# A new order of work in the first attention stage: value columns as (e, r), z on ScalarE, the product in pieces, scores, shifted products and values in groups

## What is computed

```python
xn = _ln(x, g1, b1)
q = _lin(xn, Wq, bq).reshape(b, n, H, HD) / np.sqrt(HD)
k = _lin(xn, Wk, bk).reshape(b, n, H, HD)
score = softmax(einsum('bihd,bjhd->bhij', q, k), axis=-1)
v = _lin(xn, Wv, bv).reshape(b, n, R, HD)
out = einsum('bhij,bjrd->bihrd', score, v)
qv = _lin(xn, Wqv, bqv).reshape(b, n, H, 1, QK) / np.sqrt(QK)   # broadcast over R
comp = softmax(concatenate([qv, out], -1) @ Ws.T + bs, axis=3)   # over R
out = (comp * out).sum(axis=3).reshape(b, n, DIM)
```

## Time and profile before

| | us |
|---|---|
| median of three runs (1930.48 to 1957.68) | 1944.45 |
| the profiled execution | 1938.15 |
| its span | 1936.4 |
| TensorE busy (share of the span) | 1592.3 (82%) |
| VectorE busy | 1485.4 (77%) |
| GpSimd busy | 835.4 (43%) |
| ScalarE busy | 771.2 (40%) |
| mean granted clock of TensorE, of full speed | 0.917 |

### The profile page before, as it was taken

One profiled execution on the slowest core, in us unless ns is written; L12 is line 12 of the kernel. 1 busy time (PEld: TensorE's weight loads), 2 busy tenths in 40 slices (PEclk: granted clock), 3 DMA queues, 4 the chain that ended last, 5 costly groups with the idle time before them and its releaser, 6 DMA issues. The chain is left out here.

```text
span 1936.4 us, 45555 instructions
## 1 busy us (share of the span) xinstructions
PE 1592.3 (82%) x13604; PEld 1346.0 (70%) x13668; DVE 1485.4 (77%) x3618; ACT 771.2 (40%) x1665; POOL 835.4 (43%) x1052
## 2 busy tenths in 40 slices
PE   5899898898989898999476654888888888888887
PEld 3788888888888888889355543666666666666665
DVE  4668888888888888887488865777787787777774
ACT  1345555555555555556122212333333333333331
POOL 3445554544554554453366643334333344333330
PEclk9899999999999999999689987999898999888896
DMA  3322212222122212221333312232222222222220
GB/s 110 109 85 93 79 66 70 72 80 72 65 76 73 75 64 72 73 77 42 87 94 98 98 46 73 92 99 91 90 94 97 93 92 94 90 87 88 87 93 31
DMA packets 178621, 158.08 MB, mean 82 GB/s; under 512 B 9458, under 2 KB 160114, under 8 KB 178547
## 3 DMA queue, kind: packets, MB, share of 16 engines
q1 hardware_dynamic: 178546, 157.16, 24.6%
HBM read 113.09 MB, written 44.04 MB: 81 GB/s over the span
## 5 line engine op out<-in xcount | busy, mean ns | idle before, releaser
L600 PE MATMUL a_bank<-a_vp,a_prob 128*128 128x96 f32 x4096 | 544.7, 277 | 0.3 <-ACT a_prob L457 0.3
L600 PEld LDWEIGHTS a_bank<-a_vp,a_prob 128*128 128x128 f32 x4096 | 511.3, 196 | 16.7 <-ACT a_prob L457 8.6
L633 DVE TENSOR_REDUCE a_nmax<-a_bank 128x2 f32<-128x512 f32 x512 | 331.8, 686 | 123.6 <-PE a_bank L527 123.0
L457 ACT ACTIVATE a_prob<-a_bank 128x512 f32<-128x512 f32 x512 | 306.0, 598 | 180.0 <-PE a_bank L582 170.9
L527 PE MATMUL a_bank<-a_k_st,a_q_st 96*128 96x256 bf16 x1024 | 207.8, 286 | 7.5 <-DVE a_nmax L633 5.5
L1698 DVE TENSOR_REDUCE c_nmax<-c_bank 128x4 f32<-128x512 f32 x256 | 166.8, 684 | 51.8 <-PE c_bank L1510 50.1
L1540 PE MATMUL c_o_bank<-c_vb,c_prob 128*128 128x96 f32 x1024 | 181.4, 303 | 30.0 <-DVE c_ad L1823 29.2
L582 PE MATMUL a_bank<-a_q_st,a_k_st 120*128 120x256 bf16 x1024 | 202.2, 279 | 0.0
L335 POOL TENSOR_TENSOR a_prod<-a_ov,a_wgt 128x2048 f32<-128x2048 f32 x32 | 119.0, 3719 | 144.5 <-DVE a_wgt L706 131.8
L1414 ACT ACTIVATE c_prob<-c_bank 128x256 f32<-128x256 f32 x256 | 98.8, 386 | 195.3 <-PE c_bank L1490 193.6
L1540 PEld LDWEIGHTS c_o_bank<-c_vb,c_prob 128*128 128x128 f32 x1024 | 145.9, 205 | 41.3 <-DVE c_ad L1823 29.0
(11 more groups left out here) (198 smaller groups left out, 3032.3 us busy)
## 6 DMA issues: line engine op xcount, KB each, us to landing
a_q_st<-scratch_a_parts_dram SPq DMA_DIRECT2D x192, 96.0 KB
a_k_st<-scratch_a_parts_dram SPq DMA_DIRECT2D x64, 288.0 KB
c_q_st<-scratch_c_parts_dram SPq DMA_DIRECT2D x192, 96.0 KB
c_k_st<-scratch_c_parts_dram SPq DMA_DIRECT2D x64, 288.0 KB
scratch_a_parts_dram<-a_parts SPq DMA_DIRECT2D x32, 384.0 KB, 2.7
scratch_c_parts_dram<-c_parts SPq DMA_DIRECT2D x32, 384.0 KB, 2.7
a_x<-in_x SPq DMA_DIRECT2D x32, 128.0 KB, 10.5
scratch_y<-a_y SPq DMA_DIRECT2D x32, 128.0 KB, 9.3
```

Of the source, the lines that this page charges most:

```text
L457: act.activation(prob[h % 4][:, :, :].rearrange("p a b -> p (a b)"), t_ps[h % 2][:, :], ACT.Exp).then_inc(exped, 1)
L600: mm = pe.matmul(o_ps[g % 2][:, at:at + VC], prob[h % 4][:, c, t * P:(t + 1) * P], vp[o][:, c, :], start=c == 0, stop=c == NT - 1)
L633: dve.tensor_reduce(nmax[:, t, 2 * g:2 * g + 2], s_ps[t][:, :].rearrange("p (h k) -> p h k", h=2), AX.X, ALU.max, negate=True).then_inc(ma ...
```

## The change

All in `attention_a`, lengthened here to what the prediction speaks of:

- The value columns of w_v and b_v lie as (e, r). They are loaded to a new buffer and copied in the new order by ScalarE, once. `prod` has the same order and two buffers; the product runs in four pieces with a wait behind each; the sum over r reads adjacent elements. The sums move one iteration later (batch n-4), so that the pipeline has one iteration more at its end.
- z is made by ScalarE from y and a new r2 (one GpSimd step less); x is loaded one iteration earlier.
- `OFF` 11 becomes 13, the values product comes two steps behind the shifted one, scores are spread over steps 0 to 13, `MT_AT` is (9, 15), the second copy and the second `spread` come in the next iteration; z is transposed at s = 0, q and k made at s = 2, the values of batch n-1 at s = 4.
- VectorE's non-maxima work is set between maxima; `weigh` is whole in iteration n-3; GpSimd's order is spread(1), split, norm, spread(0), product.

```diff
-        SPLIT, NORM, MP, POST = 4, 7, 8, 9
-        OFF = 11
-        S_AT = (1, 2, 3, 4, 6, 7, 8, 9)
-        MT_AT = (6, 11)
+        SPLIT, NORM, MP, POST = 4, 6, 8, 9
+        OFF, PVLAG = 13, 2
+        S_AT = (0, 0, 1, 2, 2, 3, 4, 5, 6, 7, 8, 9, 10, 11, 12, 13)
+        MT_AT = (9, 15)
+        PIECES, STAGES, FOLDED = 4, 5, 8
...
+                if active(j, u, 2):
+                    spread(1, n - 2, i)
...
-                    norm(6, pool.tensor_tensor(rt[:, 1, :], rt[:, 3, :], half[:, :], ALU.pow))
-                    norm(7, pool.tensor_tensor(r2[:, :], rt[:, 1, :], r1[:, :], ALU.mult))
+                    norm(6, pool.tensor_tensor(r2[:, :], rt[:, 3, :], half[:, :], ALU.pow))
                 if active(j, u, 1):
-                    spread(1)
+                    spread(0, n - 1, 1 - i)
+                if active(j, u, 3):
...
+                    for k in range(PIECES):
+                        gs = slice(k * H * NT // PIECES, (k + 1) * H * NT // PIECES)
+                        pool.tensor_tensor(
+                            prod[o][:, gs, :].rearrange("p g (e r) -> p g e r", r=R),
+                            ov[o][:, gs, 0:RD].rearrange("p g (e r) -> p g e r", r=R),
+                            wgt[:, gs, :].unsqueeze(2).broadcast_to([P, H * NT // PIECES, HD, R]), ALU.mult
+                            ).then_inc(prod_d, 1)
+                        pool.wait_ge(prod_d, b * PIECES + k + 1)
+                        apart(pool, spare)
...
+                    if s >= H - NT and active(j, u, -1):
+
+                        t = s - H + NT
+                        act.wait_ge(y_d, (n + 1) * NT + t + 1)
+                        if not isinstance(j, int) or n >= 1:
+                            act.wait_ge(z_t, n)
+                        act.activation(z[1 - i][:, t, :], y[1 - i][:, t, :], ACT.Copy, scale=r2[:, t:t + 1]
+                                       ).then_inc(z_d, 1)
...
+                    units = [w for w in range(H) if S_AT[w] == s] if active(j, u, 1) else []
+                    halves = [(w, hh) for w in units for hh in range(2)]
+                    for w, hh in halves:
+                        score_half(w, hh)
                     if active(j, u, lag):
...
+                        for k in range(NT):
+                            shift(n - lag, h, (i + lag) % 2, k)
+                    if active(j, u, plag):
+                        for k in range(4):
+                            values(n - plag, ph, (i + plag) % 2, k)
...
+                reduces(0, 1)
+                weighs(0, 2)
+                reduces(1, 2)
+                weighs(2, 4)
+                reduces(2, 3)
+                weighs(4, 5)
                 for k in range(MP // 2):
-                    if active(j, u, 1):
-                        split_max(1, k)
+                    if k % 2 == 0:
+                        reduces(3 + k // 2, 4 + k // 2)
                     if active(j, u, -1):
                         moments(k)
...
+                reduces(5, H // 2)
+                splits(0)
+                reduces(8, 9)
+                weighs(5, 7)
+                reduces(9, 10)
+                weighs(7, POST)
+                for t in range(NT):
+                    reduces(10 + t, 11 + t)
+                    if active(j, u, 4):
+                        summed(t)
+                if active(j, u, 1):
+                    new_values()
+                reduces(12, 14)
+                if active(j, u, -1):
                     for t in range(NT):
...
+                        normed(t)
+                reduces(14, H)
+                splits(1)
```

More of the change, by code:

```diff
@@ L419, in values_weights @@
                                bias=cols[:, 4:5]).then_inc(folded, 1)
+                act.copy(by_e(w_v[:, 0:RD]), by_r(vb_raw[:, 0, :])).then_inc(folded, 1)
+                act.copy(by_e(b_v[:, 0:RD]), by_r(vb_raw[:, 1, :])).then_inc(folded, 1)
             def body(j, u):
@@ L524, in score_unit @@
                         if w >= 2 or not isinstance(j, int) or b >= 1:
                             pe.wait_ge(maxed, b * H + w - 1)
-                        for hh in range(2):
-                            mm = pe.matmul(s_ps[t][:, hh * T:(hh + 1) * T],
-                                           q_st[o][0:MROW, 2 * g + hh, t * P:(t + 1) * P],
-                                           k_st[o][0:MROW, 2 * g + hh, :], start=True, stop=True)
+                    mm = pe.matmul(s_ps[t][:, hh * T:(hh + 1) * T],
+                                   q_st[o][0:MROW, 2 * g + hh, t * P:(t + 1) * P],
+                                   k_st[o][0:MROW, 2 * g + hh, :], start=True, stop=True)
@@ L530, in score_unit, with shift @@
+                    if hh:
                         mm.then_inc(score, 1)
+                def shift(b, h, o, c):
+                    if c == 0:
+                        if isinstance(b, int) and b < 2 and h == 0:
+                            pe.wait_ge(ones_d, 2 * (b + 1))
+                        if h % (H // 2) == 0:
+                            pe.wait_ge(m_in[h // (H // 2)], b + 1)
+                        if h >= 2 or not isinstance(j, int) or b >= 1:
+                            pe.wait_ge(exped, b * H + h - 1)
+                    mm = pe.matmul(t_ps[h % 2][:, c * T:(c + 1) * T],
+                                   k_st[o][0:AROWS, h, c * P:(c + 1) * P], q_st[o][0:AROWS, h, :],
+                                   start=True, stop=True)
+                    if c:
+                        mm.then_inc(shifted, 1)
@@ new lines, in values @@
+                def values(b, h, o, k):
+                    g, t, c = h // 2, k // NT, k % NT
+                    if k == 0:
+                        pe.wait_ge(exped, b * H + h + 1)
+                        if h == 0:
+                            pe.wait_ge(v_d, b + 1)
+                        if h % 2 == 0 and (g >= 2 or not isinstance(j, int) or b >= 1):
+                            pe.wait_ge(ov_d, b * (H // 2) + g - 1)
+                    at = (2 * (h % 2) + t) * VC
+                    mm = pe.matmul(o_ps[g % 2][:, at:at + VC], prob[h % 4][:, c, t * P:(t + 1) * P],
+                                   vp[o][:, c, :], start=c == 0, stop=c == NT - 1)
+                    if k == 3:
+                        mm.then_inc(pv, 1)
@@ new lines, in weighs, with splits @@
+                def weighs(lo, hi):
+                    if active(j, u, 3):
+                        for k in range(lo, hi):
+                            weigh(k, n - 3, 1 - i)
+                def splits(half_):
+                    if active(j, u, 1):
+                        for k in range(MP // 2):
+                            split_max(half_, k)
+                reduces(0, 1)
[3 more added lines that the diff above has]
+                reduces(2, 3)
```

265 lines of the change are left out of this document (113 added, 152 removed).

## The result

| | before | after |
|---|---|---|
| median, us (4 runs each) | 1951.07 (1930.48 to 1958.89) | 1976.86 (1970.37 to 1984.8) |
| profiled execution / span | 1938.15 / 1936.4 | 1970.37 / 1968.6 |
| VectorE busy | 1485.4 | 1428.8 |
| mean granted clock | 0.917 | 0.889 |

The ratio is 1.0147, 95% interval 1.0086 to 1.0207: slower, clear of noise, by less than 2%. The forecast was 1916 with a range to 1965: wrong in sign and outside its range. The time is that of the rival called slower (1972).

What follows compares the result with a forecast made beforehand. VectorE and TensorE wait for each other in turn, nobody full. Iteration 27.28 to 26.4 us saves 0.9 x 28 = 25, ends add 3: 1938.15 - 25 + 3 = 1916 us, range 1866 to 1965.

Steps and rivals of the forecast that it cites:

- the rival called slower: Two TensorE stops, for the split and z, make the half clock last to q and k: 1972 us; chance 0.15.
- TensorE's need: TensorE's work in one attention A iteration without any wait: 22.8 us, against 27.28 us measured before.
- the walk: One changed iteration timed from z's transpose: waits 0.7 us at w4, 1.5 at the second split, 0.8 for z; 26.4 total.
- The low clock is hidden here: Half clock behind TensorE's 1.5 us stop costs 1.5 us, which falls on the waits for z and w4.
- 0.9 us x 28 = 25 us: Gain over attention A's full iterations: 27.28 - 26.4 = 0.9 us each, 28 iterations.
- Without scores in groups nothing in this sum changes: Grouping a step's products on TensorE is worth 0, bounds 0 and 0.2 us a step, since products stream either way.
- z on ScalarE: Moving z takes 0.5 us off VectorE (bounds 0 and 0.84); on ScalarE two instructions of 0.28 us.
- Sum over r: VectorE's two sums fall from 2.01 to 1.22 us each, 1.6 us a batch off VectorE.
- Pieces: GpSimd's product in four pieces of 1.05 us with 0.2 between: 4.8 us, against 3.72 in one.
- Ends: The last batch: 3.3 us for more steps, product 1.1 longer, sums 1.6 shorter: +3 us.
- DMA: Loads of stacked scores: stack there at 23.5 us, 2.9 before its use, so hidden but not far.
- the rival without it: Faster: y and splits aren't held by GpSimd's pieces; iteration 24.35 us, 82 us less, 1859; chance 0.33.

Runs made afterwards that it cites:

- experiment 1: Changed kernel plus eight unused identity products on TensorE at step 15, ahead of the wait for the second split of maxima: 1934.32 us, ratio 0.9948.
- Experiment 2: Kernel before the change plus seven unused identity products ahead of TensorE's wait for z: 1932.59 us, ratio 0.988.
- experiment 5: Changed kernel with the products of a step in turn again instead of all scores, then all shifted products: 1924.66 us, ratio 0.9876.
- Experiment 4: Changed kernel with z back on VectorE behind y and the seventh small norm step on GpSimd: 1946.64 us, ratio 0.9981.
- experiment 8: Changed kernel with the old (r, e) column order in w_v, b_v, the product and the sum: 1940.62 us, ratio 0.9974.
- the kernels with 24.3 to 24.5 us an iteration: Changed kernel with the second maxima transposed next iteration (1862.39 us); also with z ahead of exp (1865.90), or y early and products in turn (1857.07).
- experiment 7: Changed kernel with both y ahead of the second spread and the four pieces: 1947.26 us, ratio 1.0.
- experiment 9: Changed kernel with the second half's maxima transposed at step 1 of the next iteration, their copy behind xn: 1862.39 us, ratio 0.9626.
- the kernels of the table: The kernel before, the changed kernel and seven variants of it, compared by waits and low-clock stretches; 26.76 to 29.20 us an iteration.

## Why the prediction was wrong

*TensorE's need and the walk: right.* I forecast 26.4 us from one z to the next at full clock; with the stop filled it is 26.76. Term by term, in us from z, in the iteration of the timeline above (z at 510.10) and in one of experiment 1 (z at 493.57):

| | walk | after | experiment 1, full clock |
|---|---|---|---|
| y begins | 19.6 | 20.1 | 19.1 |
| first piece | 18.75 | 20.1 | 19.1 |
| last piece ends | 23.55 | 25.4 | 24.4 |
| second split begins / ends | 22.8 / 24.3 | 23.0 / 25.6 | 22.0 / 24.6 |
| TensorE reaches step 15 / goes on | 22.8 / 24.3 | 23.5 / 25.8 | filled / 24.8 |
| border to the next z | 2.1 | 2.0 | 2.0 |
| next z | 26.4 | 27.7 | 26.75 |

The iteration after the change began at the lower clock, and that is 1.0 us in each of its lines against experiment 1. What is left against the walk is in the pieces (1.18 for my 1.05): four of them are 0.5 us. The casts are held as the walk said, by two pieces instead of one.

*"The low clock is hidden here": the step that failed.* I let the clock be 0.50 behind the stop for as long as before and covered it by the waits for z and w4. The stretches became twice as long in 13 of 17 cases. They last up to q and k (z at 537.82, q loaded at 543.59, clock low until 544.2) or end just ahead of them (z at 567.36, low until 571.4, q at 572.31), where I had let the low clock fall on the waits for z and w4 alone. The waits that were to cover them are smaller than I had them: at full clock, in experiment 1, the wait that the walk has at w4 is 0.4 us and not 0.7, the one for z 0.5 and not 0.8:

```profile
PE a_bank L547 <- DVE a_nmax L669: 6.9, 17, 0.4
```

After the change the first is gone from the waits and the second is 4.8 / 16 = 0.3 on the mean, so the low clock was covered for 0.6 us and not for 1.5. Between full clock and this it is 28.62 - 26.76 = 1.9 us an iteration, 52 over 28; the stop filled gave back 43 (39 by the ratios). My slower rival had the low clock reaching to q and k, and 1972 us; that the second stop is what makes it last, as the rival says, the rows don't bear out (see behind the table), so its number is right with a reason that is open in part. I gave it 0.15, "since the stops here are each shorter". They were not: 1.5 forecast, 2.2 measured, against 1.85 before.

*The comparison was uneven.* 27.28 of before contains its low clock, 26.4 does not. My reading of 1.5 us behind each wait was too much besides: a low stretch follows 11 of 17 waits and makes the iteration 27.6 instead of 26.64, 0.64 us on the mean. Experiment 2 sets them side by side: 26.63 against 26.76. "0.9 us x 28 = 25 us" was a gain against the clock only.

*"Without scores in groups nothing in this sum changes": wrong.* Not the products' own time, which I looked at, but where y falls beside the first piece: 1.5 us an iteration at full clock, and 52 us in all with the low clock that comes or doesn't (experiment 5).

*z on ScalarE: wrong in sign.* I booked a gain of 0.5 us on VectorE and left the place to the border. The border was right to 0.1 us. Experiment 4 without it is 30 us faster and has short stretches of low clock in place of long ones; the way from the one to the other stays open.

*Sum over r: right in size* (1.22 forecast, 1.21 measured), *wrong in what it is worth*: in this order it makes the kernel slower by 36 us (experiment 8), all of it by the clock, since work that VectorE is spared in the middle only makes TensorE come earlier to a split whose end the pieces set.

*Pieces:* 1.05 would have been right for the old column order (1.073); in the new one 1.183, beyond the bound of 1.15 that I had from a row of the same size in plain order. *Ends:* +3 forecast; from the last transpose of z (865.2, now 881.8) to the end of the last sum of the stage 72.3 us before and 80.4 now, +8; which of the terms is the larger one wasn't looked at. *DMA:* hidden, as said; it shows as a wait that counts only in the kernels with 24.3 to 24.5 us an iteration; the walk had 23.5 for the stack.

*The rule of the Trainium skill* ("GPSIMD Engine Reference", Specifications: GpSimd and VectorE share their SBUF interface, and instructions with two SBUF inputs or in a 2-port mode collide) was the right choice against the rival without it: y and the split are held in nearly every iteration. y and the casts have one input; whether they run in such a mode no run here shows. Which instruction is held is in these rows a matter of when it starts: the casts in one order, the two-input ones in another (1.10 and 0.18 after the change, 0.17 and 1.11 in experiment 7).

The gains are not additive: each of experiments 1, 4, 5, 7 and 8 gives back 29 to 53 us by the ratios, and in the profiles all of them have less of the same thing, the low clock at the border (a granted clock of 0.94 to 1.00 on the mean from 400 to 860 instead of 0.89).

## What to carry to other kernels

Compare two schedules at the same clock before asking what a change gives: a few idle products in the stop tell in one run how much of a difference is work and how much is the clock. Ask of each saving on another engine whether it shortens TensorE's stop or only gathers several small stops to a long one, and of each instruction moved off an engine whether it now stands behind the very wait that it should avoid. Where a chain of small instructions ends beside another engine's long ones, it paid more here to ask for its result later (experiment 9) than to make it faster (experiment 7).

## What the runs showed of the hardware that I had not expected

- The low clock comes in two lengths. In the kernels of the table the stretches below 0.9 are up to 4 windows of 1 us or 7 to 8, with none between. The stop's length doesn't tell which, or whether one comes: the same wait of 1.85 us for z in the kernel before was followed by a low stretch in 11 of 17 iterations, a stop of 2.6 us alone gave the short one in 16 of 17, one of 2.2 us after the change the long one in 13 of 17, with or without a second wait.
- The column order that makes VectorE's sum faster (2.01 to 1.21 us) makes GpSimd's product slower: 1.073 to 1.183 us for 512 elements, 3.72 to 4.20 for 2048 in one instruction. The product then reads the weights repeated in the middle dimension instead of in the innermost; which of its operands costs the time wasn't tried.
- The casts, the two-input instructions and y, where they began with one of GpSimd's pieces or 0.1 us behind it, ended with the piece, however small they were: 16 elements took 1.10 us beside a piece, two y of 0.3 us each took 4.50 beside the whole product. The maxima, read from PSUM, were not held (0.68 us on the mean, as before).
